# Taking full tiles and end tiles of the expert stage in turns from place 36 on

## The chip, the cores and the metric

The kernel runs on one core of one Trainium2 chip. The metric is the device time of one execution in microseconds; a smaller number is better. The engines are TensorE (PE, with its weight loads shown as PEld), VectorE (DVE), ScalarE (ACT), GpSimd (POOL) and SyncE (SP), which only issues transfers.

## What is computed

A graph network layer on 32 graphs of 256 nodes (8192 tokens, 128 features) is followed by a feed-forward layer with 8 experts, of which each token uses two. The second half is what the change touches:

```python
logits = jnp.einsum('bsd,de->bse', xn, Wr) + br
top_vals, top_idx = jax.lax.top_k(logits, K)            # K = 2
w = jax.nn.softmax(top_vals, axis=-1)
w_full = jnp.einsum('bsk,bske->bse', w, jax.nn.one_hot(top_idx, E, dtype=w.dtype))
for e in range(E):                                       # E = 8, H = 256, D = DOUT = 128
    h = jax.nn.gelu(jnp.einsum('bsd,dh->bsh', xn, W1[e]) + b1[e], approximate=False)
    y_e = jnp.einsum('bsh,hd->bsd', h, W2[e]) + b2[e]
    y = y + y_e * w_full[..., e, None]
```

## The kernel before

**Routing.** A token's two experts make a class; there are 28 classes. In the first stage (16 groups of 512 tokens) the graph layer and the router run, and every token's row (normalised features, residual, shares, its own number) is scattered to `rows_dram`, sorted by class. Each class then consists of full tiles of 128 rows and one end tile, which is filled up with idle rows.

**Places.** The expert stage goes through 92 places, one tile each: places 0 to 63 are slots for full tiles (`NT`), places 64 to 91 the end tiles of the 28 classes (`NC`). The first 20 (`EARLY`) start while the last two groups are still being routed; from place 20 on the tables are complete. The class of an end tile is known when the program is built. The class of a full tile is data: four of them are packed in one 24-bit word, which PE, ACT and DVE load into a register at every fourth full tile (`value_load`), and from which `expert` computes the addresses of weights, biases and shares with register instructions.

**One step.** All engines run a loop over steps, each written out in the program's order:

- SP loads the rows of place i into one of 26 buffers (line 428), once the result of place i - 26 has been sent. Behind every second load from place 21 to 47 it also writes the idle rows of one class's end tile (`fill_end`, line 432); those of the first 14 classes are written before place 20. Before place 64 it waits for all 28 (`fill_sent`).
- PE transposes the tile of place i (line 785), does the wide product of place i - 2 (four matmuls, line 805) and the narrow one of place i - 4 (four matmuls, line 822). There are three banks for narrow products, so the narrow product of place m waits for the result of place m - 3.
- ACT copies the weights of a full tile to fixed buffers (lines 946 and 950), moves the transposed tile (line 955) and applies gelu (line 962). An end tile needs no copy, since PE reads its weights in place.
- DVE, in this order: first bias of place i (line 1545), first product of place i - 4 (line 1559), second bias of place i (line 1566), second product of place i - 4 (line 1573, the result). The word for place i is loaded at line 1540, that for place i - 4 at line 1551; as 4 is also the number of tiles in a word, both loads fall in the same step.
- POOL scatters the result to `out` (line 572) and, up to place 85, clears a scratch tile behind it (line 528).

Of the kernel before, what the change touches and what calls it, by code (L numbers as in the profile page):

```python
# [8 lines left out]
P = 128  # L9
# [5 lines left out]
NT = NTOK // P  # L15
# [7 lines left out]
NC = len(PAIRS)  # L23
# [29 lines left out]

BACK = D + E

XR, XD, AR, RO, HR = 6, 3, 3, 8, 8
STEPS = NG + 3
RING, SENDS = 26, 18
# [40 lines left out]
    return rows  # L99


def expert(words, i, width, low):

    if i >= NT:
        return PAIRS[i - NT][0 if low else 1] * width
    word = words[i // PER_WORD % 2]
    at = 6 * (i % PER_WORD) + (0 if low else 3)
    shift = width.bit_length() - 1 - at
    if shift > 0:
        taken = (word & (E - 1) << at) << shift  # L110
    else:
        taken = (word >> -shift) & (E - 1) * width
    return taken.with_bounds(min_val=0, max_val=(E - 1) * width)


def build(nc, x, x_t, adj_t, eps, gw1, gb1, rms_w, gw2, gb2, gamma, beta, wr, br, w1, b1, w2, b2,
          fixed_in, idle_in, out):
    fixed_at = constants()[1]
    with ExitStack() as ctx:
# [3 lines left out]
        def sem(name):  # L123
            return ctx.enter_context(nc.semaphore(name))
# [211 lines left out]
        columns_turned = sem("columns_turned")  # L336
        table_ready = sem("table_ready")
        ends_ready = sem("ends_ready")
        fill_sent = sem("fill_sent")
        idle_sent = sem("idle_sent")  # L340

        rows_here = [sem(f"rows_here{k}") for k in range(RING)]
# [45 lines left out]

        def highs_placed(i):

            return sum(high_by_gpsimd(m) == high_by_gpsimd(i) for m in range(i + 1))

        block = ctx.enter_context(nc.Block())

        @block.sync
        def _(sp):
            def load_features(g):
                if g >= XD:
                    sp.wait_ge(x2_ready, g - XD + 1)
                sp.dma_start(x_d[:, g % XD], x_t[:, g * GT:(g + 1) * GT]).then_inc(x_d_in[g % XD], 16)  # L400

            for g in range(NG):
                if g == XR:
                    for dst, src in expert_loads:
                        sp.dma_start(dst, src).then_inc(weights_in, 16)
                if g >= XR:
                    sp.wait_ge(xn1_ready, g - XR + 1)
                if g == 2:
                    sp.wait_ge(adj_in[1], 16)
                sp.dma_start(x_tok[:, g % XR], x_view[g]).then_inc(x_in[g % XR], 16)  # L410
                if g >= AR:
                    sp.wait_ge(agg_done, g - AR + 1)
                if g == 1:
                    sp.wait_ge(adj_in[0], 16)
                sp.dma_start(adj[:, g % AR], adj_view[g]).then_inc(adj_in[g % AR], 16)
                if g >= 4:
                    load_features(g - 4)
            for g in range(NG - 4, NG):
                load_features(g)

            def load_rows(i):
                if i < NT:
                    start = sp.value_load(first_row[0:1, i:i + 1], min_val=0, max_val=IDLE + (NC - 1) * P)
                else:
                    start = sp.value_load(left_row[0:1, i - NT:i - NT + 1], min_val=0, max_val=IDLE + (NC - 1) * P)
                if i >= RING:
                    sp.wait_ge(result_sent[(i - RING) % SENDS], 16 * ((i - RING) // SENDS + 1))
                sp.dma_start(rows_in[:, i % RING], rows_dram[bass.ds(start, P), :]).then_inc(rows_here[i % RING], 16)

            def fill_end(c):  # L430
                end = sp.value_load(end_row[0:1, c:c + 1], min_val=0, max_val=IDLE + (NC - 1) * P)
                sp.dma_start(rows_dram[bass.ds(end, P), :], idle_in[c * P:(c + 1) * P]).then_inc(fill_sent, 16)

            sp.wait_ge(table_ready, 1)
            for k, n in enumerate(sent_before(KNOWN)):
                sp.wait_ge(rows_sent[k], 16 * TPG * n)
            for i in range(EARLY):
                load_rows(i)

            sp.wait_ge(ends_ready, 1)
            for c in range(NC // 2):
                fill_end(c)
            sp.wait_ge(table_ready, 3)
            sp.wait_ge(idle_sent, 16)
            for k, n in enumerate(sent_before(NG - 1)):
                sp.wait_ge(rows_sent[k], 16 * TPG * n)
            for i in range(EARLY, NT):
                load_rows(i)  # L450
                if i % 2 and i - EARLY < NC:
                    fill_end(NC // 2 + (i - EARLY) // 2)
            sp.wait_ge(fill_sent, 16 * NC)
            for i in range(NT, TILES):
                load_rows(i)

        @block.gpsimd
        def _(pool):
# [163 lines left out]
        def _(pe):  # L622
# [157 lines left out]
            def tile_step(step):  # L780
# [7 lines left out]
                if (i := tile_at(step, WIDE_LAG)) is not None:  # L788
                    pe.wait_ge(xg_t_ready, i + 1)
                    if (m := before_in_bank(H_BANKS, i)) is not None:  # L790
                        pe.wait_ge(gelu_done, m + 1)
                    for w, now in enumerate((w1_low, w1_high)):
                        if i >= NT:
                            now_at = expert({}, i, HE, w == 0)
                            w1_now = w1_sb[:, now_at:now_at + HE]
                        else:
                            w1_now = now[:, i % 4]
                            if w == 0:
                                pe.wait_ge(low_placed, i + 1)
                            elif high_by_gpsimd(i):  # L800
                                pe.wait_ge(high_placed2, highs_placed(i))
                            else:
                                pe.wait_ge(high_placed, highs_placed(i))
                        for c in range(HCE):
                            last = pe.matmul(h_ps(i)[:, w * HCE + c], w1_now[:, c * P:(c + 1) * P], xg_t[:, i % 4],  # L805
                                             start=True, stop=True)
                    last.then_inc(h_done, 1)
                    tail(step, 1)
                if (i := tile_at(step, NARROW_LAG)) is not None:
                    if i < NT and i % PER_WORD == 0:  # L810
                        words[i // PER_WORD % 2] = pe.value_load(word[0:1, i // PER_WORD:i // PER_WORD + 1], min_val=0,
                                                                 max_val=2 ** 24 - 1)
                    pe.wait_ge(gelu_done, i + 1)
                    if (m := before_in_bank(Y_BANKS, i)) is not None:
                        pe.wait_ge(result_ready, m + 1)
                    for w in range(2):
                        if i < EARLY:
                            bias_at = expert(words, i, D, w == 0)
                            pe.matmul(y_ps(i)[:, w], bias_sel[:], b2_parts[:, bass.ds(bias_at, D)], start=True, stop=False)
                        at = expert(words, i, HE, w == 0)  # L820
                        for c in range(HCE):
                            last = pe.matmul(y_ps(i)[:, w], hidden_e[:, i % 4, w * HCE + c],  # L822
                                             w2_sb[:, bass.ds(at + c * D, D)], start=(c == 0 and i >= EARLY),
                                             stop=(c == HCE - 1))
                    last.then_inc(y_done, 1)
                    tail(step, 2)
# [13 lines left out]
        def _(act):  # L840
# [97 lines left out]
            def place_weights(i):  # L938
                if i >= 4:
                    act.wait_ge(h_done, i - 3)  # L940
                if i < NT:
                    if i % PER_WORD == 0:
                        words[i // PER_WORD % 2] = act.value_load(word[0:1, i // PER_WORD:i // PER_WORD + 1],
                                                                  min_val=0, max_val=2 ** 24 - 1)
                    at = expert(words, i, HE, True)
                    nc.scalar.activation(w1_low[:, i % 4], w1_sb[:, bass.ds(at, HE)], ACT.Copy
                                         ).then_inc(low_placed, 1)
# [40 lines left out]
        def _(dve):  # L988
# [544 lines left out]
            def tile_step(step):  # L1533
# [2 lines left out]
                    i = None  # L1536
                if i is not None:
                    rows = rows_in[:, i % RING]
                    if i < NT and i % PER_WORD == 0:
                        words[i // PER_WORD % 2] = dve.value_load(word[0:1, i // PER_WORD:i // PER_WORD + 1],  # L1540
                                                                  min_val=0, max_val=2 ** 24 - 1)
                    dve.wait_ge(rows_here[i % RING], 16 * (i // RING + 1))
                    if i >= AHEAD:
                        dve.wait_ge(result_ready, i - AHEAD + 1)
# [2 lines left out]
                                                   rows[:, X2_AT:X2_AT + D], ALU.mult, ALU.add).then_inc(based, 1)  # L1547
                tail(step, 0)
                if j is not None:
                    if j < NT and j % PER_WORD == 0:  # L1550
                        done_words[j // PER_WORD % 2] = dve.value_load(word[0:1, j // PER_WORD:j // PER_WORD + 1],
                                                                       min_val=0, max_val=2 ** 24 - 1)
                    done = rows_in[:, j % RING]
                    if j >= EARLY:
                        dve.wait_ge(base_done, j - EARLY + 1)
# [65 lines left out]
```

## Time and profile before

| | |
|---|---|
| median of 3 runs | 411.95 us (411.73 to 412.13) |
| time of the profiled execution | 411.64 us |
| its span, first to last instruction | 409.9 us |
| mean granted TensorE clock | 0.995 |
| TensorE busy (weight loads) | 382.9 us (326.3 us) |
| VectorE busy | 301.2 us |
| ScalarE busy | 277.7 us |
| GpSimd busy | 314.2 us |

The profiled execution is 0.31 us below the median, and 1.7 us of it lie outside the span. A busy TensorE says only that some matmul is in flight; whether it runs at its pace is read from the starts of equal instructions one tile apart.

### The profile page before, as it was taken

Reading aid. Unit: us, or ns where it says so; the run is one execution under the profiler, and the core shown is the slowest. Engines: PE = TensorE matmul, PEld = TensorE weight load, DVE = VectorE, ACT = ScalarE, POOL = GpSimd, SP = SyncE. Lnnn points to the kernel's source line nnn. Section 1 sums busy time; section 2 is a strip of 40 time slices with the busy share of each in tenths; the row PEclk is TensorE's granted clock in tenths of the full one; section 3 lists DMA queues with packets and bytes.
Section 4 is the critical chain, followed back from the end, with each engine's and each line's share of the span. In section 5 each row is a group of like instructions: output and inputs, shape, how many; then the busy total and the mean of one; then the engine's idle time right before and its main releaser. Section 6 shows DMA issues by size and latency. Waiting matters only on the chain. (4 is left out here: it accounts for less than half of the span.)

```text
span 409.9 us, 11327 instructions
## 1 busy us (share of the span) xinstructions
PE 382.9 (93%) x2598; PEld 326.3 (80%) x2598; DVE 301.2 (73%) x1290; ACT 277.7 (68%) x653; POOL 314.2 (77%) x440
## 2 busy tenths in 40 slices
PE   1899999999999999999789996999999999999994
PEld 1467777767777777777569996999999899999993
DVE  5687789999999999998865752566666666765562
ACT  1377777787778898779878554677777776555540
POOL 1223378877787899888888879997787677999984
PEclk9999999999999999999999999899999999999999
DMA  7879974444423442221266355555555544331111
GB/s 227 259 242 337 338 232 137 141 144 142 139 88 115 156 144 79 76 69 55 68 157 180 111 156 140 158 150 153 145 153 156 156 124 110 108 87 40 38 38 38
DMA packets 43472, 57.25 MB, mean 140 GB/s; under 512 B 6224, under 2 KB 36176, under 8 KB 42768
## 3 DMA queue, kind: packets, MB, share of 16 engines
q1 hardware_dynamic: 35200, 36.74, 32.4%
q0 software_dynamic: 6096, 18.52, 12.9%
q10 hardware_dynamic: 2112, 1.27, 1.1%
q8 instruction: 24, 0.39, 0.4%
q14 instruction: 40, 0.33, 0.3%
HBM read 41.80 MB, written 22.31 MB: 156 GB/s over the span
## 5 line engine op out<-in xcount | busy, mean ns | idle before, releaser
L572 POOL DMA_INDIRECT out<-result,rows_in x92 | 90.3, 981 | 27.8 <-DVE result L1573 15.8
L822 PE MATMUL banks<-w_sb,hidden_e 128*128 (+1 forms) x736 | 102.7, 281 | 2.8 <-DVE result L1573 2.4
L822 PEld LDWEIGHTS banks<-w_sb,hidden_e 128*128 128x128 f32 x736 | 92.2, 193 | 4.7 <-issue 4.2
L962 ACT ACTIVATE hidden_e<-banks 128x512 f32<-128x512 f32 x92 | 54.9, 597 | 45.4 <-PE banks L805 43.6
L515 POOL DMA_INDIRECT rows_dram<-rows_out,row_of x64 | 65.3, 1021 | 13.4 <-issue 10.6
L649 PE MATMUL banks<-gw_sb,agg 128*128 128x512 f32 x128 | 65.2, 595 | 0.9 <-DVE gw_sb L1013 0.9
L673 PE MATMUL banks<-hidden_t,gw_sb 128*128 128x256 f32 x256 | 62.3, 386 | 1.7 <-ACT hidden_t L885 1.7
L528 POOL MEMSET space<- 128x620 f32 x100 | 63.0, 630 | 0.1
L673 PEld LDWEIGHTS banks<-hidden_t,gw_sb 128*128 128x128 f32 x256 | 46.4, 190 | 16.1 <-ACT hidden_t L885 7.3
L1108 DVE TENSOR_TENSOR hidden<-banks,rms_bc 128x512 f32<-128x512 f32 x64 | 43.8, 685 | 15.3 <-ACT hidden L870 15.1
L955 ACT ACTIVATE xg_t<-banks,ones 128x128 f32<-128x128 f32 x92 | 33.3, 362 | 22.0 <-PE banks L785 21.9
L878 ACT ACTIVATE hidden<-hidden,rrms 128x512 f32<-128x512 f32 x64 | 45.8, 717 | 0.1
L1559 DVE SCALAR_TENSOR_TENSOR acc<-banks,rows_in,acc 128x128 f32<-128x128 f32 x72 | 25.2, 351 | 26.9 <-PE banks L822 19.5
L870 ACT ACTIVATE hidden<-banks 128x512 f32<-128x512 f32 x64 | 38.2, 596 | 9.6 <-PE banks L649 7.8
L637 PE MATMUL banks<-adj,xn 128*128 128x256 f32 x128 | 32.3, 398 | 9.2 <-DVE xn L1089 9.2
L885 ACT ACTIVATE hidden_t<-banks 128x512 f32<-128x512 f32 x64 | 38.0, 594 | 3.1 <-PE banks L660 2.9
L805 PE MATMUL banks<-xg_t,w_low 128*128 128x128 f32 x256 | 39.7, 278 | 0.0
L660 PEld LDWEIGHTS banks<-fixed,hidden 128*128 128x128 f32 x256 | 30.4, 141 | 11.5 <-issue 6.6
L805 PE MATMUL banks<-xg_t,w_high 128*128 128x128 f32 x256 | 39.1, 275 | 0.0
L660 PE MATMUL banks<-fixed,hidden 128*128 128x128 f32 x256 | 38.9, 275 | 0.1
L1545 DVE SCALAR_TENSOR_TENSOR acc<-b_bc,rows_in 128x128 f32<-128x128 f32 x72 | 25.1, 349 | 15.9 <-DVE result L1573 13.4
L469 POOL TENSOR_TENSOR rstd<-var,minus_half 128x4 f32<-128x4 f32 x16 | 16.9, 1056 | 26.0 <-DVE var L1081 25.7
(148 smaller groups left out, 741.2 us busy)
## 6 DMA issues: line engine op xcount, KB each, us to landing
rows_in<-rows_dram SPq DMA_DIRECT2D x92, 132.5 KB, 2.3
adj<-adj_t SPq DMA_DIRECT2D x16, 512.0 KB, 5.0
x_tok<-x SPq DMA_DIRECT2D x16, 256.0 KB, 6.1
x_d<-x_t SPq DMA_DIRECT2D x16, 256.0 KB, 4.8
rows_dram<-idle_in POOLq DMA_DIRECT2D x1, 3710.0 KB, 13.9
rows_dram<-idle_in SPq DMA_DIRECT2D x28, 132.5 KB
out<-result,rows_in POOLq DMA_INDIRECT x92
w_sb<-w SPq DMA_DIRECT2D x1, 1024.0 KB, 8.3
```

The source lines that it names most:

```text
L515: nc.gpsimd.indirect_dma_start(out=rows_dram, out_offset=bass.IndirectOffsetOnAxis(ap=row_of[:, g * TPG + t:g * TPG + t + 1], axis=0), in_ ...
L528: nc.gpsimd.memset(space[:], 0.0).then_inc(spaced, 1)
L572: nc.gpsimd.indirect_dma_start(out=out, out_offset=bass.IndirectOffsetOnAxis(ap=rows_in[:, i % RING][:, IDX_AT:IDX_AT + 1].bitcast(U32), a ...
L649: pe.matmul(hid_ps[:, n % 3], agg[:, g % 2, t * P:(t + 1) * P], gw1_sb[:], start=True, stop=True).then_inc(hid_done, 1)
L660: last = pe.transpose(hidt_ps[t % 2][:, c * P:(c + 1) * P], hidden[:, n % HR, c * P:(c + 1) * P], ident)
L673: last = pe.matmul(z_ps[:, cols], gw2_sb[:, c], hidden_t[:, g % 2, c, cols], start=(c == 0), stop=(c == HC1 - 1))
L805: last = pe.matmul(h_ps(i)[:, w * HCE + c], w1_now[:, c * P:(c + 1) * P], xg_t[:, i % 4], start=True, stop=True)
L822: last = pe.matmul(y_ps(i)[:, w], hidden_e[:, i % 4, w * HCE + c], w2_sb[:, bass.ds(at + c * D, D)], start=(c == 0 and i >= EARLY), stop=( ...
L870: nc.scalar.activation(hidden[:, n % HR], hid_ps[:, n % 3], ACT.Square, scale=H1 ** -0.5, accum_out=sumsq[:, g % 2, t:t + 1]).then_inc(sum ...
L878: nc.scalar.activation(hidden[:, n % HR], hidden[:, n % HR], ACT.Silu, scale=rrms[:, g % 2, t:t + 1]).then_inc(silu_done, 1)
L962: nc.scalar.activation(hidden_e[:, i % 4], h_ps(i), ACT.Gelu).then_inc(gelu_done, 1)
L1108: nc.vector.tensor_tensor(hidden[:, n % HR], hid_ps[:, n % 3], rms_bc[:], ALU.mult).then_inc(weighted, 1)
```

## The change

The order of the tiles is mapped: places 0 to 35 are full tiles as before; from place 36 (`TURNS`) on, even places take the full tiles 36 to 63 and odd places the end tiles 0 to 27. A word is loaded when a full tile with a number divisible by four comes up, which is at every eighth place from 36 on. The waits for placed weights count full tiles only. The wait for the idle rows is split in halves: the first 14 classes' before the load of place 37, the others' before that of place 65.

```diff
+TURNS = TILES - 2 * NC
+def tile_of(i):
+    if i < TURNS:
+        return i
+    k = (i - TURNS) // 2
+    return NT + k if (i - TURNS) % 2 else TURNS + k
 def expert(words, i, width, low):
+    i = tile_of(i)
     if i >= NT:
...
-        fill_sent = sem("fill_sent")
+        fill_sent = [sem(f"fill_sent{k}") for k in range(2)]
...
-            return sum(high_by_gpsimd(m) == high_by_gpsimd(i) for m in range(i + 1))
+            return sum(high_by_gpsimd(m) == high_by_gpsimd(i) for m in range(i + 1) if tile_of(m) < NT)
+        def lows_placed(i):
+            return sum(tile_of(m) < NT for m in range(i + 1))
+        def new_word(i):
+            t = tile_of(i)
+            return t // PER_WORD if t < NT and t % PER_WORD == 0 else None
...
             def load_rows(i):
-                if i < NT:
-                    start = sp.value_load(first_row[0:1, i:i + 1], min_val=0, max_val=IDLE + (NC - 1) * P)
+                t = tile_of(i)
+                if t < NT:
+                    start = sp.value_load(first_row[0:1, t:t + 1], min_val=0, max_val=IDLE + (NC - 1) * P)
...
-            for i in range(EARLY, NT):
+            for i in range(EARLY, TILES):
+                for k in range(2):
+                    if tile_of(i) == NT + k * NC // 2:
+                        sp.wait_ge(fill_sent[k], 16 * (NC // 2))
                 load_rows(i)
                 if i % 2 and i - EARLY < NC:
                     fill_end(NC // 2 + (i - EARLY) // 2)
-            sp.wait_ge(fill_sent, 16 * NC)
-            for i in range(NT, TILES):
-                load_rows(i)
...
-                        if i >= NT:
+                        if tile_of(i) >= NT:
...
-                                pe.wait_ge(low_placed, i + 1)
+                                pe.wait_ge(low_placed, lows_placed(i))
...
-                    if i < NT and i % PER_WORD == 0:
-                        words[i // PER_WORD % 2] = dve.value_load(word[0:1, i // PER_WORD:i // PER_WORD + 1],
-                                                                  min_val=0, max_val=2 ** 24 - 1)
+                    if (k := new_word(i)) is not None:
+                        words[k % 2] = dve.value_load(word[0:1, k:k + 1], min_val=0, max_val=2 ** 24 - 1)
```

The last replacement is made in the same way for PE, for ACT and for the second load on DVE.

## Rows read from the trace of the kernel before

**Rows 1.** Busy us (x instructions) of PE, PEld, DVE, ACT, POOL; then clock, DMA share, GB/s.

```profile
268.19:287.15 18.96, 18.96 (x173) 18.96 (x171) 13.05 (x38) 14.82 (x40) 15.73 (x21) 1.00 0.54 151
...
287.15:345.19 58.04, 55.37 (x479) 53.98 (x477) 39.24 (x113) 42.17 (x112) 44.55 (x56) 1.00 0.53 143
...
345.19:396.38 51.19, 51.19 (x462) 51.19 (x461) 33.02 (x114) 26.04 (x54) 46.53 (x58) 1.00 0.23 67
```

**Rows 2.** Timeline of TensorE: starts of single transposes, one at each place.

```profile
287.15 0.27 PE L785 MATMUL banks<-fixed,rows_in 128*128 128x128 f32 x1
...
292.84 0.27 PE L785 MATMUL banks<-fixed,rows_in 128*128 128x128 f32 x1
...
295.11 0.27 PE L785 MATMUL banks<-fixed,rows_in 128*128 128x128 f32 x1
...
297.16 0.27 PE L785 MATMUL banks<-fixed,rows_in 128*128 128x128 f32 x1
...
300.96 0.27 PE L785 MATMUL banks<-fixed,rows_in 128*128 128x128 f32 x1
...
303.58 0.27 PE L785 MATMUL banks<-fixed,rows_in 128*128 128x128 f32 x1
...
305.48 0.27 PE L785 MATMUL banks<-fixed,rows_in 128*128 128x128 f32 x1
...
345.19 0.27 PE L785 MATMUL banks<-fixed,rows_in 128*128 128x128 f32 x1
...
396.38 0.27 PE L785 MATMUL banks<-fixed,rows_in 128*128 128x128 f32 x1
```

**Rows 3.** Waits between 285 and 345 us: in total, times, longest.

```profile
PE banks L822 <- DVE result L1573: 2.4, 5, 0.5
```

**Rows 4.** Timeline of VectorE, steps in which both tiles are full.

```profile
293.33 0.35 DVE L1573 SCALAR_TENSOR_TENSOR result<-banks,rows_in,acc 128x128 f32<-128x128 f32 x1
...
333.28 0.35 DVE L1545 SCALAR_TENSOR_TENSOR acc<-b_bc,rows_in 128x128 f32<-128x128 f32 x1 [0.62 <-DVE result L1573]
...
334.19 0.35 DVE L1559 SCALAR_TENSOR_TENSOR acc<-banks,rows_in,acc 128x128 f32<-128x128 f32 x1 [0.56 <-issue]
...
335.54 0.35 DVE L1545 SCALAR_TENSOR_TENSOR acc<-b_bc,rows_in 128x128 f32<-128x128 f32 x1 [0.17 <-DVE result L1573]
...
337.32 0.35 DVE L1545 SCALAR_TENSOR_TENSOR acc<-b_bc,rows_in 128x128 f32<-128x128 f32 x1 [0.21 <-DVE result L1573]
...
339.10 0.35 DVE L1545 SCALAR_TENSOR_TENSOR acc<-b_bc,rows_in 128x128 f32<-128x128 f32 x1 [0.21 <-DVE result L1573]
...
341.67 0.35 DVE L1545 SCALAR_TENSOR_TENSOR acc<-b_bc,rows_in 128x128 f32<-128x128 f32 x1 [1.00 <-DVE result L1573]
```

**Rows 5.** Timeline of VectorE, one step in which both are end tiles.

```profile
353.36 0.34 DVE L1545 SCALAR_TENSOR_TENSOR acc<-b_bc,rows_in 128x128 f32<-128x128 f32 x1
...
354.54 0.34 DVE L1545 SCALAR_TENSOR_TENSOR acc<-b_bc,rows_in 128x128 f32<-128x128 f32 x1
```

**Rows 6.** VectorE's register load of line 1551: ns min/median/max, first and last start.

```profile
L1551 DVEq TENSOR_LOAD <-word x16: 298/304/661, 213.5 to 348.8; - x16
```

**Rows 7.** Timeline of SyncE: start, length of the run of issues, their count.

```profile
232.33 18.29 SPq L432 DMA_DIRECT2D rows_dram<-idle_in  x14
...
280.24 1.45 SPq L428 DMA_DIRECT2D rows_in<-rows_dram  x2
...
300.38 0.59 SPq L432 DMA_DIRECT2D rows_dram<-idle_in  x1
```

**Rows 8.** Timeline of GpSimd: two sends of results.

```profile
380.46 1.10 POOL L572 DMA_INDIRECT out<-result,rows_in  x1 [0.17 <-DVE result L1573]
...
394.83 0.97 POOL L572 DMA_INDIRECT out<-result,rows_in  x1 [0.17 <-issue]
```

**Rows 9.** Timeline of the end: last result and last send.

```profile
404.29 0.35 DVE L1573 SCALAR_TENSOR_TENSOR result<-banks,rows_in,acc 128x128 f32<-128x128 f32 x1
...
405.89 0.97 POOL L572 DMA_INDIRECT out<-result,rows_in  x1 [0.30 <-DMA out<-result,rows_in]
```

More of the change, by code:

```diff
@@ L421, in load_rows @@
             def load_rows(i):
-                if i < NT:
-                    start = sp.value_load(first_row[0:1, i:i + 1], min_val=0, max_val=IDLE + (NC - 1) * P)
+                t = tile_of(i)
+                if t < NT:
+                    start = sp.value_load(first_row[0:1, t:t + 1], min_val=0, max_val=IDLE + (NC - 1) * P)
                 else:
-                    start = sp.value_load(left_row[0:1, i - NT:i - NT + 1], min_val=0, max_val=IDLE + (NC - 1) * P)
+                    start = sp.value_load(left_row[0:1, t - NT:t - NT + 1], min_val=0, max_val=IDLE + (NC - 1) * P)
                 if i >= RING:
@@ L431, in fill_end @@
                 end = sp.value_load(end_row[0:1, c:c + 1], min_val=0, max_val=IDLE + (NC - 1) * P)
-                sp.dma_start(rows_dram[bass.ds(end, P), :], idle_in[c * P:(c + 1) * P]).then_inc(fill_sent, 16)
+                sp.dma_start(rows_dram[bass.ds(end, P), :], idle_in[c * P:(c + 1) * P]).then_inc(fill_sent[c // (NC // 2)], 16)
             sp.wait_ge(table_ready, 1)
@@ L809, in tile_step @@
                 if (i := tile_at(step, NARROW_LAG)) is not None:
-                    if i < NT and i % PER_WORD == 0:
-                        words[i // PER_WORD % 2] = pe.value_load(word[0:1, i // PER_WORD:i // PER_WORD + 1], min_val=0,
-                                                                 max_val=2 ** 24 - 1)
+                    if (k := new_word(i)) is not None:
+                        words[k % 2] = pe.value_load(word[0:1, k:k + 1], min_val=0, max_val=2 ** 24 - 1)
                     pe.wait_ge(gelu_done, i + 1)
@@ L940, in place_weights @@
                     act.wait_ge(h_done, i - 3)
-                if i < NT:
-                    if i % PER_WORD == 0:
-                        words[i // PER_WORD % 2] = act.value_load(word[0:1, i // PER_WORD:i // PER_WORD + 1],
-                                                                  min_val=0, max_val=2 ** 24 - 1)
+                if tile_of(i) < NT:
+                    if (k := new_word(i)) is not None:
+                        words[k % 2] = act.value_load(word[0:1, k:k + 1], min_val=0, max_val=2 ** 24 - 1)
                     at = expert(words, i, HE, True)
@@ L1538, in tile_step @@
                     rows = rows_in[:, i % RING]
-                    if i < NT and i % PER_WORD == 0:
-                        words[i // PER_WORD % 2] = dve.value_load(word[0:1, i // PER_WORD:i // PER_WORD + 1],
-                                                                  min_val=0, max_val=2 ** 24 - 1)
+                    if (k := new_word(i)) is not None:
+                        words[k % 2] = dve.value_load(word[0:1, k:k + 1], min_val=0, max_val=2 ** 24 - 1)
                     dve.wait_ge(rows_here[i % RING], 16 * (i // RING + 1))
@@ L1549, in tile_step @@
                 if j is not None:
-                    if j < NT and j % PER_WORD == 0:
-                        done_words[j // PER_WORD % 2] = dve.value_load(word[0:1, j // PER_WORD:j // PER_WORD + 1],
-                                                                       min_val=0, max_val=2 ** 24 - 1)
+                    if (k := new_word(j)) is not None:
+                        done_words[k % 2] = dve.value_load(word[0:1, k:k + 1], min_val=0, max_val=2 ** 24 - 1)
                     done = rows_in[:, j % RING]
```

## The prediction

> **What bounds the kernel now.** I read the page first: TensorE is busy 93% of the span, which hides whether it runs at its pace. So the next view is the timeline of TensorE, of the transposes alone, since there is one for each place. The last one, at 396.38 us, is place 91, and 27 before it, at 345.19, is place 64, the first end tile [rows 2]. That is 51.19 us for 27 places, 1.896 us each. Another 28 back stands place 36, at 287.15: 58.04 us for 28 full tiles, 2.073 each. The reader is to see two regimes on one engine. In the second, weight loads fill the whole stretch (51.19 of 51.19 us) at granted clock 1.00 [rows 1]: TensorE's own pace. Full tiles alone can reach it too: the stretch before place 36 (268.19 to 287.15) holds ten places in 18.96 us, at the same clock [rows 1]. So a full tile isn't dearer for TensorE, and after place 36 something holds it up: 58.04 - 28 x 1.896 = 4.95 us.
>
> The view of the waits names DVE's result as what TensorE's narrow products waited for, five times, 2.4 us [rows 3]; the weight loads behind such a wait are late as well, which that line doesn't count. The starts show where: place 39 to 40 takes 2.27 us instead of 1.896, 40 to 41 takes 2.05, 43 to 44 takes 2.62, and then 44 to 45 is 1.90 again [rows 2]. In step 39 the narrow product of place 35 is due, which needs the result of place 32; in step 43 that of place 39, which needs result 36. Both results come from steps in which DVE loads its two words.
>
> DVE's timeline gives the price. A step with two full tiles and no word takes 1.78 us (337.32 to 339.10). The one with the words has 0.62 us of idle time before line 1545 and 0.56 before line 1559, where the others have 0.21 and next to nothing. Four steps with one word step take 341.67 - 333.28 = 8.39 us [rows 4], that is 2.10 a tile, against TensorE's 4 x 1.896 = 7.58. DVE is the bound among full tiles, by its register work, although it counts as busy for only 39.24 of 58.04 us. It starts with some places in hand (three banks), so TensorE feels it only from step 39 on. Among end tiles a step of DVE takes 354.54 - 353.36 = 1.18 us [rows 5], and it waits for TensorE in every one. So DVE binds for 28 places and idles for the next 28.
>
> **The change, part by part.** *DVE.* No instruction on data is added or removed; the register work of 28 full tiles is spread over 56 places. The lag of four places between the two halves of a step is even, so from place 40 on both halves are full or both are end tiles. Eight steps are then four full ones, with two word loads as now, and four end ones: 8.39 + 4 x 1.18 = 13.11 us. TensorE needs 8 x 1.896 = 15.17. DVE gains 2.06 us in eight steps, 0.26 a step, where it now loses 0.20 among full tiles. The two loads no longer meet: place 36, 44, 52 and 60 bring line 1540's, and steps 40, 48, 56 line 1551's, so each word step has one of about half the extra time; only in step 36 do both fall together (tile 36 and tile 32). One load takes 304 ns on DVE [rows 6].
>
> *Where the gain begins.* Steps up to 36 are the same instructions. Step 36 has both loads, and result 32 is ready as late as before (started 293.33 [rows 4]), so the 2.27 us before place 40 stays: place 40 starts at 295.11 again. From there the next word step must not stall. DVE's steps 37 and 39 have one full half and one end half (between 1.18 and 1.78, middle 1.48), 38 is full, 40 is full with one word (1.78 and half of the two loads' 1.0, so 2.3): 7.04 us from result 32 to result 36. TensorE takes 7.58 over four places, so result 36 is 0.5 us earlier against its need than result 32, which was late by 2.27 - 1.90 = 0.37. It now takes DVE 8.39. No stall is left after 40; the little one to place 41 (2.05 - 1.90 = 0.15) stays or goes.
>
> *TensorE.* From place 40 to 91 there are 51 intervals. At 1.896: 295.11 + 96.7 = 391.81 us for the last transpose instead of 396.38, 4.57 earlier. If the small stall stays, 4.42; if the first goes as well, 4.95.
>
> *ACT.* It copies weights for every second place only. Ten full tiles in a row at TensorE's pace cost it 14.82 us busy in 18.96 [rows 1], so it isn't the bound even at twice that density.
>
> *SP.* Its queue keeps the order of loads and fills; only the row addresses differ, and the waits for the idle rows move. The wait before place 37 is for the 14 fills issued from 232.33 to 250.62, thirty microseconds earlier. The other 14 end with the one at 300.38 [rows 7], behind the load of place 47, and are asked for before that of place 65, which can't be issued before result 39 is out anyway. Cost nothing; what hides it: the pair of loads 36 and 37 is issued at 280.24, so place 37's at about 281.0, lands 2.3 us later by the page, and is used at 287.15 + 1.90 = 289.05. 5.7 us of cover.
>
> *POOL.* It sends one result a place. 0.17 idle, 0.97 send and 0.63 clearing (the page's mean for line 528) make 1.77 us [rows 8], below 1.896. It keeps up. In one stretch, though, the send takes 1.10 us, and then 1.90 is just TensorE's pace.
>
> The Trainium skill, "SBUF — State Buffer", section "Who interferes with whom", says that a DVE instruction with two inputs in SBUF contends with a GpSimd instruction that reads SBUF, and not with one that only writes. DVE's bias steps are of that kind, and they will come more evenly than now. By the row of 0.97 the sum has no term for POOL; by the rule POOL would be as in the stretch of 1.10, which the rival below prices. This trace bears the rule out no further than 1.10 beside 0.97.
>
> *The end.* Now 13.5 us lie between the last transpose and the end of the span; the last result starts at 404.29 and its send at 405.89 [rows 9]. After the change places 88 and 90 are full, so DVE does register work for two of its four instructions there: between nothing (it waits for TensorE before them) and half of 1.78 - 1.18 = 0.3 each. I take 0.1 in all.
>
> Sum: 411.64 - 4.57 + 0.1 = 407.17 us for a profiled execution, and 0.31 more to the median of the runs: 407.5 us.
>
> **The rivals.**
>
> *The lag stays for some rounds.* If mixed steps cost DVE as much as full ones (1.78), result 36 comes 7.64 us after result 32 and the late place isn't made good; one or two of the stalls of 2.62 - 1.90 = 0.72 are left, at 43 to 44 and at 51 to 52. For it: the pieces of idle time that the profile puts down to nothing. Against it: 0.26 gained a step. Time 408.9 with two left.
>
> *It is TensorE's own word load.* TensorE loads every word too, and this count stays. Then seven stalls of 0.72 stay, and nothing is gained: 412. Against it: its load for tile 40 is in step 44, and place 44 to 45 takes 1.90 us; the stall stands one step earlier. Also its loads for tiles 24 and 28, in steps 28 and 32, fell in the stretch at full pace [rows 1].
>
> *POOL has no slack.* If its sends take 1.10 us from place 40 on, its period is 1.90, it never works off a lag, and up to one period stands before the last sends: between 407.5 and 409.3, some 408.5. Against it: it went back to 0.97 by itself [rows 8], and the last six sends have no clearing behind them. The skill's rule named under POOL speaks for it.
>
> *Slower: an end tile's load blocks SP.* All loads from 37 on and the second 14 fills stand behind the wait before place 37. It decides only if the first fills land after 281.0 + 5.7 = 286.7, and makes the kernel slower if after 286.7 + 4.5 + 0.8 = 292.0: 41 us after the last was issued. The page's slowest transfer of idle rows, 3710 KB, takes 13.9. If it happened, at 44 us say, 415.
>
> **How the numbers follow.** My forecast, own range 406.6 to 408.3 (bounds: both stalls gone, 407.1, less some noise; small stall left and 0.6 at the end, 408.2): 0.75. Lag for some rounds 0.11, POOL 0.08, TensorE's own load 0.03, blocked SP 0.03. The range takes in the first three as far as 409.2: 406.4 to 409.2. Within 0.2% of 411.95 is 411.1 to 412.8, about what a measurement can tell from no change. Faster 0.94, same 0.03, slower 0.03.
>
> **What would show it.** Right: transposes 1.90 us apart from place 40 to 91, the last at about 391.8; no wait of line 822 for line 1573 after about 296 us; DVE waiting for line 822 from some place after 44 on; word steps with one long idle piece instead of two. Wrong: intervals of 2.6 every eight places (TensorE's own load, or ACT late with its copies), POOL never waiting for a result in the last 30 us, or a hole at place 37 with "rows_in" as its releaser. What would make it wrong most easily: a cost of changing between kinds of tiles that no row here shows, as none here has both kinds in turn; DVE's mean step of 1.64 would pass 1.896 only if each change cost over 0.26 us.

## The result, and the profile after

The changed kernel took 408.07 us (median of 6 runs, 407.16 to 409.66) against 412.21 for the kernel before (6 runs, 411.73 to 412.53): ratio 0.991, 95% interval 0.9891 to 0.9928. Forecast were 407.5 us in a range of 406.4 to 409.2. It is faster. These six runs scatter more than those of before; in a later round (the last table of the experiments) the two kernels scatter alike, over 3.0 and 2.8 us.

The profiled execution took 408.06 us, with a span of 406.2. The windows of the changed kernel (columns as in [rows 1]) show the same three kinds of stretch; line 806 is now the transpose, 842 the narrow product, 1563, 1576, 1583 and 1590 DVE's four instructions in their order, 593 the send.

```profile
264.55:287.83 23.28, 23.00 (x206) 22.82 (x205) 14.97 (x44) 18.19 (x49) 21.12 (x28) 1.00 0.54 150
287.83:341.36 53.53, 53.41 (x478) 53.22 (x477) 37.31 (x118) 34.61 (x85) 48.56 (x61) 1.00 0.55 154
295.86:392.55 96.69, 96.69 (x870) 96.69 (x868) 65.70 (x209) 62.73 (x153) 84.73 (x106) 1.00 0.39 111
```

The last one is places 40 to 91: weight loads fill all of its 96.69 us. The timeline of TensorE, transposes alone (places 35, 36, 39, 40, 91):

```profile
285.40 0.27 PE L806 MATMUL banks<-fixed,rows_in 128*128 128x128 f32 x1
...
287.83 0.27 PE L806 MATMUL banks<-fixed,rows_in 128*128 128x128 f32 x1
...
293.58 0.27 PE L806 MATMUL banks<-fixed,rows_in 128*128 128x128 f32 x1
...
295.86 0.27 PE L806 MATMUL banks<-fixed,rows_in 128*128 128x128 f32 x1
...
392.55 0.27 PE L806 MATMUL banks<-fixed,rows_in 128*128 128x128 f32 x1
```

392.55 - 295.86 = 96.69 us for 51 places, 1.896 each: none of the stalls of [rows 2] is left behind place 40. The 28 places from 36 to 64 take 341.36 - 287.83 = 53.53 us instead of 58.04. Place 39 to 40 takes 2.28, as before. New is place 35 to 36: 2.43 us instead of 1.90.

The waits of the changed kernel between 285 and 345 us have no row any more in which line 842 waits for DVE's result [rows 3]. That alone proves little, since the two stalls before places 36 and 40 lie in this window and the view puts them down to nothing ("issue", the second line below); the starts above are what shows them, and that none follows. The order of waiting has turned round, DVE waits for TensorE:

```profile
DVE acc L1576 <- PE banks L842: 4.8, 10, 0.9
...
PEld banks L842 <- issue: 0.8, 2, 0.5
```

DVE's own steps while it catches up (timeline of VectorE; steps 41 to 44 begin with these rows, 41 and 43 are end steps, 42 a full one):

```profile
301.13 0.34 DVE L1563 SCALAR_TENSOR_TENSOR acc<-b_bc,rows_in 128x128 f32<-128x128 f32 x1
...
302.31 0.35 DVE L1563 SCALAR_TENSOR_TENSOR acc<-b_bc,rows_in 128x128 f32<-128x128 f32 x1
...
303.81 0.34 DVE L1563 SCALAR_TENSOR_TENSOR acc<-b_bc,rows_in 128x128 f32<-128x128 f32 x1
...
305.41 0.35 DVE L1563 SCALAR_TENSOR_TENSOR acc<-b_bc,rows_in 128x128 f32<-128x128 f32 x1 [0.48 <-issue]
```

1.18 us for an end step, as in [rows 5]; 303.81 - 302.31 = 1.50 us for a full one, less than the 1.78 of [rows 4]. The word for step 44 is loaded in the 0.48 us before its first instruction, alone: the other load is gone from that step.

One send that took longer, and the end (the last result and its send; before: [rows 9]):

```profile
391.32 1.11 POOL L593 DMA_INDIRECT out<-result,rows_in  x1 [0.72 <-DVE result L1590]
...
400.75 0.35 DVE L1590 SCALAR_TENSOR_TENSOR result<-banks,rows_in,acc 128x128 f32<-128x128 f32 x1
...
402.23 0.98 POOL L593 DMA_INDIRECT out<-result,rows_in  x1 [0.30 <-issue]
```

From the last transpose to the end of the span pass 406.2 - 392.55 = 13.65 us, before 13.5.

### The profile page after: what moved, and what is told of

Its sections match the earlier page's. It is cut to its first block and busy times, and to the rows that moved or that the text cites. A ratio compares the mean times of both kernels' runs of the same rounds, so it can differ in the third digit from the quotient of the medians.

```text
span 406.2 us, 11327 instructions
## 1 busy us (share of the span) xinstructions
PE 381.3 (94%) x2598; PEld 325.6 (80%) x2598; DVE 300.4 (74%) x1290; ACT 277.6 (68%) x653; POOL 314.4 (77%) x440
## 5 line engine op out<-in xcount | busy, mean ns | idle before, releaser
L536 POOL DMA_INDIRECT rows_dram<-rows_out,row_of x64 | 65.5, 1023 | 13.5 <-issue 10.7
L658 PEld LDWEIGHTS banks<-adj,xn 128*128 128x128 f32 x128 | 25.2, 199 | 14.3 <-issue 8.1
```

Of the source, the lines that this page charges most:

```text
L536: nc.gpsimd.indirect_dma_start(out=rows_dram, out_offset=bass.IndirectOffsetOnAxis(ap=row_of[:, g * TPG + t:g * TPG + t + 1], axis=0), in_ ...
L658: last = pe.matmul(agg_ps[:, b * NODES:(b + 1) * NODES], xn1[:, g % 2, 2 * b + c], adj[:, g % AR, 2 * b + c], start=(c == 0), stop=(c == 1))
```

## The experiments

Most runs are compared by TensorE's transposes rather than by their times. The times carry a scatter that arises ahead of the places concerned: from place 8 to place 24, where the last groups are routed and the tables built, the profiles below take between 41.3 and 45.5 us, whatever the kernel. The kernel before itself took 412.21, 414.26, 408.99 and 412.46 us in the four rounds of runs (6, 7, one and 11 executions), so a time is compared only with that of the kernel before in the same round. b_peload (round of 414.26) and a_pad1, a_pad3, a_endsfirst and a_blocks14 (round of 408.99) ran once each. All sums in this table are differences of starts of transposes in the profiled execution; the last column is from the last transpose to the end of the span. At TensorE's pace places 24 to 91 would take 67 x 1.896 = 127.0 us.

| kernel | time of this execution | places 8 to 24 | 24 to 36 | 36 to 64 | 64 to 91 | 24 to 91 | behind |
|---|---|---|---|---|---|---|---|
| before | 411.64 | 41.88 | 22.75 | 58.04 | 51.19 | 131.98 | 13.5 |
| changed | 408.06 | 41.76 | 23.28 | 53.53 | 51.19 | 128.00 | 13.65 |
| changed, again (a_again) | 409.06 | 41.74 | 24.32 | 53.61 | 51.18 | 129.11 | 13.7 |
| before, words loaded once (b_reuse) | 406.94 | 42.83 | 22.96 | 53.09 | 51.18 | 127.23 | 13.5 |
| the same again (b_reuse_again) | 406.33 | 41.58 | 22.75 | 53.15 | 51.19 | 127.09 | 13.4 |
| before, more loads on TensorE (b_peload) | 415.96 | 45.53 | 23.23 | 57.87 | 51.23 | 132.33 | 13.7 |
| changed, words loaded once (a_reuse) | 409.85 | 44.72 | 23.24 | 53.08 | 51.19 | 127.51 | 13.5 |
| turns from place 20 (a_turns20) | 408.71 | 43.03 | 22.75 | 53.08 | 51.19 | 127.02 | 14.0 |
| 1 more in each end step (a_pad1) | 406.58 | 41.54 | 22.75 | 53.46 | 51.19 | 127.40 | 13.6 |
| 3 more in each end step (a_pad3) | 408.28 | 42.33 | 22.75 | 53.45 | 51.19 | 127.39 | 13.9 |
| 28 end tiles, then 28 full (a_endsfirst) | 411.43 | 42.36 | 22.75 | 53.08 | 52.11 | 127.94 | 16.6 |
| blocks of 14 (a_blocks14) | 408.59 | 41.66 | 22.75 | 56.07 | 51.18 | 130.00 | 13.5 |
| all together (a_best) | 406.12 | 41.26 | 23.34 | 53.09 | 51.18 | 127.61 | 13.4 |

**Is it DVE's register work? (b_reuse)** The order stays as before; only the word of a full tile is kept from the step in which DVE first needs it.

```diff
                         words[i // PER_WORD % 2] = dve.value_load(...)
+                        kept[i // PER_WORD] = words[i // PER_WORD % 2]
...
                     if j < NT and j % PER_WORD == 0:
-                        done_words[j // PER_WORD % 2] = dve.value_load(...)
+                        if j < EARLY:
+                            done_words[j // PER_WORD % 2] = dve.value_load(...)
+                        else:
+                            done_words[j // PER_WORD % 2] = kept[j // PER_WORD]
```

> The kernel before, but from place 20 on VectorE loads each word once: the word that line 1540 loads for place i is kept for the same tile four steps later, so line 1551's load goes. Theory (VectorE's register work bounds the full tiles): a group of four full steps falls from 8.39 us by about 0.5 to 7.9, still above TensorE's 7.58; the stalls of 2.6 us at every fourth place fall to 1.9 to 2.3, places 36 to 64 take about 54.5 instead of 58.0 us, and the time is 2.5 to 3.5 us below the kernel before. Rival (TensorE's own word load, or anything outside VectorE, makes the stalls): no change within 0.3 us.

Measured: places 36 to 64 in 53.09 us, all intervals from place 34 to 91 at 1.90; 408.09 us (median of 4) against 414.26 of the kernel before on that chip, ratio 0.9872 (0.9825 to 0.9918). The rival is out: nothing but DVE's register work was touched, and every stall behind place 34 went (one of 0.2 us is left ahead of it, before place 32). I had the size wrong, since I took one load off and nothing more. The sequencer's records of line 1559 before and of its successor, line 1563, in the second run of this kernel:

```profile
L1559 DVEq ALU_OP  x112: 40/45/57, 216.4 to 353.4; - x112
```

```profile
L1563 DVEq ALU_OP  x35: 40/45/57, 216.2 to 264.3; - x35
```

112 register instructions became 35, and the last of these is at 264.3 us, before any of the full tiles concerned; line 1577 (the result) went from 128 to 40. With one register for both halves, the addresses computed for a tile in its first half serve again in its second. Four results in a row (timeline of VectorE, the second run):

```profile
292.36 0.35 DVE L1577 SCALAR_TENSOR_TENSOR result<-banks,rows_in,acc 128x128 f32<-128x128 f32 x1
...
293.87 0.34 DVE L1577 SCALAR_TENSOR_TENSOR result<-banks,rows_in,acc 128x128 f32<-128x128 f32 x1
...
295.90 0.34 DVE L1577 SCALAR_TENSOR_TENSOR result<-banks,rows_in,acc 128x128 f32<-128x128 f32 x1
...
297.82 0.35 DVE L1577 SCALAR_TENSOR_TENSOR result<-banks,rows_in,acc 128x128 f32<-128x128 f32 x1
```

The first pair lies in steps without a word and without a wait: 1.51 us for a full step instead of 1.78. The last pair spans a step with its word, 1.92 us; between them DVE waits for TensorE. That makes 3 x 1.51 + 1.92 = 6.45 us for four, below TensorE's 7.58 by far, where I had expected 7.9, and the time fell by 6 us on that chip instead of 2.5 to 3.5. The profiles show 4.75 us of it (places 24 to 91, 131.98 to 127.23); they don't show where the rest lies.

**Is it TensorE's own load of the word? (b_peload)**

```diff
                         words[i // PER_WORD % 2] = pe.value_load(word[0:1, i // PER_WORD:i // PER_WORD + 1], ...)
+                    if EARLY <= i < NT and i % PER_WORD == 2:
+                        words[i // PER_WORD % 2] = pe.value_load(word[0:1, i // PER_WORD:i // PER_WORD + 1], ...)
```

> The kernel before with one more load of the same word into a register on TensorE for every four full tiles from place 20 on (11 more loads). Theory: TensorE's own load is hidden, the intervals stay at 2.6 us once in four places and the time stays within 0.5 us of the kernel before. Rival (TensorE's own word load makes the stall): a second stall of about 0.7 us in each group, 4 to 7 us slower.

The eleven loads were made, 303 ns each:

```profile
L814 PEldq TENSOR_LOAD <-word x11: 297/303/308, 271.0 to 352.6; - x11
```

Places 24 to 91 took 132.33 us against 131.98 before, and 36 to 64 even 57.87 against 58.04. Seven stalls more would have been 5 us. TensorE's load is hidden. (Its time of 415.96 is high because places 8 to 24 took 3.7 us longer; that part is the same code.) This kernel, in the order of before, also shows a stall, 2.38 us from place 35 to 36, so such a stall doesn't need the turns. It has added loads ahead of that place, though, so it is not quite the kernel before.

**What is left for DVE in the changed kernel? (a_reuse, a_turns20)** The first keeps the words as above in the changed kernel. The second begins the mixing at place 20 (`tile_of(i)` then returns `ORDER[i]`, here and in the orders further down):

```diff
-TURNS = TILES - 2 * NC
+FULLS, ENDS = list(range(EARLY, NT)), list(range(NT, TILES))
+ORDER = list(range(EARLY))
+while FULLS or ENDS:
+    late = len(ENDS) * (NT - EARLY) > len(FULLS) * NC
+    ORDER.append((ENDS if late or not FULLS else FULLS).pop(0))
```

> The changed kernel with the same saving on VectorE. Theory: VectorE is no bound from place 40 on, so nothing is gained there; only the stalls before place 36 and 40 (2.43 and 2.28 instead of 1.90 us) go, since VectorE goes through places 20 to 36 with less register work: 0.5 to 1.0 us below the changed kernel. Rival (VectorE still bounds the stage in turns): 2 us or more below.

> The changed kernel with the mixing begun at place 20 instead of 36: 44 full and 28 end tiles spread evenly over places 20 to 91. Theory: VectorE never falls behind, the stalls at places 36 and 40 go, every interval from about place 25 on is 1.90 us: 0.8 to 1.1 us below the changed kernel. Rival (those two intervals have another cause, such as instruction fetch): no change. Rival (irregular order costs something): slower than the changed kernel.

Measured: 408.0 us (ratio 0.9849, 0.9801 to 0.9896) and 407.3 us (0.9836, 0.9792 to 0.9881), both against 414.26. In both profiles places 36 to 64 take 53.08 us, which is 28 x 1.896, so the stall before place 40 is gone as expected, and so is that before place 36. But a_reuse has two others further ahead, 2.06 us before place 29 and 2.22 before place 31, which make its 23.24 us for places 24 to 36. By places 24 to 91 a_reuse is 0.5 us below the changed kernel and a_turns20 1.0. With turns from place 20 places 24 to 91 take 127.02 us, TensorE's pace throughout. Behind the last transpose a_turns20 takes 14.0 us, 0.4 more than the changed kernel: its place 91 is a full tile.

**How much slack has DVE in turns? (a_pad1, a_pad3)** In every end step behind place 40 (26 of them, one more than the expectation counts) DVE gets 1 or 3 instructions more:

```diff
+                if i is not None and i > 40 and tile_of(i) >= NT:
+                    ...
+                    for n in range(3):
+                        last = nc.vector.scalar_tensor_tensor(pad[:, n], b2_bc[:, 0:D], rows[:, W_AT:W_AT + 1],
+                                                              rows[:, X2_AT:X2_AT + D], ALU.mult, ALU.add)
```

> The changed kernel with one more VectorE instruction (the form of line 1545, static addresses, result never used) in each of the 25 steps from 43 on whose tile is an end tile. Theory: VectorE needs 13.11 us for eight steps where TensorE needs 15.17; one more instruction an end step adds 4 x 0.26 = 1.04, 14.15 in all, still below. Places 24 to 91 take 128.0 us as in the changed kernel, within 0.3. Rival (VectorE sets the pace in the stage in turns): 25 x 0.26 = 6.5 us longer.

> The same with three such instructions in each end step. Theory: 13.11 + 12 x 0.26 = 16.23 us for eight steps, 1.06 more than TensorE's 15.17; over the 49 places from 43 on 6.5 us, less the places that VectorE may lag behind (three banks, 2 to 4 us): places 24 to 91 take 2.5 to 5 us longer than in the changed kernel, and TensorE's intervals are uneven (1.90 and over 2.1) again in the last third. If VectorE has more slack than I reckon, no change.

One more costs nothing, as expected (127.40). Three more cost nothing either (127.39), where I had expected 2.5 to 5 us. The timeline of VectorE in that run, the starts of steps 46 and 54 and between them the three instructions of step 47 in one row:

```profile
310.43 0.35 DVE L1565 SCALAR_TENSOR_TENSOR acc<-b_bc,rows_in 128x128 f32<-128x128 f32 x1
...
312.19 0.89 DVE L1573 SCALAR_TENSOR_TENSOR pad<-b_bc,rows_in 128x128 f32<-128x128 f32 x3
...
325.25 0.35 DVE L1565 SCALAR_TENSOR_TENSOR acc<-b_bc,rows_in 128x128 f32<-128x128 f32 x1
```

Eight steps take 325.25 - 310.43 = 14.82 us, with twelve instructions more at 0.26, and fit below TensorE's 15.17. Without them it is 11.7 us, not my 13.11. The surplus is in the full steps: 1.50 us in turns, 1.78 among themselves. Probably the register instructions of a full step run while the four instructions of the end step before it, which need none, are still being worked off; that reading no run tests.

**Is it turns that matter, or DVE's lag? (a_blocks14, a_endsfirst)** The two orders, with the numbers written out:

```diff
-TURNS = TILES - 2 * NC
+ORDER = list(range(36)) + list(range(64, 92)) + list(range(36, 64))      # a_endsfirst
+ORDER = [*range(50), *range(64, 78), *range(50, 64), *range(78, 92)]     # a_blocks14
```

> The changed kernel with another order from place 36 on: all 28 end tiles, then full tiles 36 to 63. Theory: the 28 end tiles run at 1.90 and let VectorE catch up; the full tiles then start without a lag, VectorE loses 0.2 us a tile, and TensorE feels it only after its slack of some 3 to 4 us is used, after 15 to 20 tiles: 1.5 to 3 us of stalls at the end, 1.5 to 3 us slower than the changed kernel in places 24 to 91, and 2 to 3.5 faster than before. Rival (a stretch of full tiles costs the same wherever it stands): as slow as before, 4 us slower than the changed kernel.

> From place 36 on 14 full, 14 end, 14 full, 14 end tiles. Theory: the first 14 full tiles follow 16 others, so the lag is there already, and their stalls stay (about 0.75 at every fourth place, 2.5 us in all); in the second block VectorE starts without a lag and 14 x 0.2 = 2.8 us stays within the slack, no stall. Places 24 to 91 take 1.5 to 2.5 us longer than in the changed kernel. Rival (what matters is only that the kinds take turns one by one): 4 us longer.

In blocks of 14 the first block of full tiles (places 36 to 49) has the stalls of before: 2.27, 2.05, 2.63, 2.79 and 2.69 us at places 40, 41, 44, 48 and 52, 3.0 us in all over the pace. The second block of 14 full tiles has none. Places 24 to 91 take 2.0 us longer than in the changed kernel, as expected. With the end tiles first, full tiles run at 1.90 for 20 places and stall at 84, 88 and 89, for 0.9 us together; 1.5 to 3 was too much. But 3 us came where I had not looked. The end of that run:

```profile
394.59 1.28 PE L839 MATMUL banks<-w_sb,hidden_e 128*128 x8 [0.39 <-DVE result L1587]
...
400.26 1.15 PE L839 MATMUL banks<-w_sb,hidden_e 128*128 x8 [0.71 <-DVE result L1587]
...
401.86 1.15 PE L839 MATMUL banks<-w_sb,hidden_e 128*128 x8 [0.45 <-DVE result L1587]
...
404.07 0.35 DVE L1587 SCALAR_TENSOR_TENSOR result<-banks,rows_in,acc 128x128 f32<-128x128 f32 x1 [0.29 <-DVE acc L1573]
...
405.69 0.98 POOL L590 DMA_INDIRECT out<-result,rows_in  x1 [0.31 <-DMA out<-result,rows_in]
```

The last narrow products wait for DVE's results (0.39, 0.71, 0.45), and 16.6 us pass behind the last transpose instead of 13.5. A lag that is within the slack of three banks costs nothing in mid-stage and is paid nearly in full at the end: result 87 starts 6.45 us after the transpose of place 91, in the kernel before 2.69, and the last result comes 3.1 us later behind that transpose than there. So the rival (a stretch of full tiles costs the same wherever it stands) falls for the places. With the end counted, places 24 to 91 and what is behind them take 144.5 us, 2.9 more than in the changed kernel, as expected, but only 1.0 less than in the kernel before, where 2 to 3.5 were expected. The time itself shows no gain at all: 411.43 us, against 408.99 for the kernel before in the same round, one execution each, which the scatter of places 8 to 24 can cover.

**Side by side on one chip (a_again, b_reuse_again, a_best).** a_best has turns from place 20, words loaded once, and end tiles in the last four places.

```diff
+ORDER, LAST = list(range(EARLY)), 4
+while FULLS:
+    late = (len(ENDS) - LAST) * (NT - EARLY) > len(FULLS) * (NC - LAST)
+    ORDER.append((ENDS if late else FULLS).pop(0))
+ORDER += ENDS
```

> The changed kernel once more, unaltered, on one chip with the next two. Expected: about 1% below the kernel before, as in its first runs; in its profile places 40 to 91 at 1.90 us each, places 24 to 91 in 127.4 to 128.1 us.

> The order before with every word loaded once on VectorE, unaltered from its first run. If the whole gain is VectorE's register work, this kernel and the changed one come out the same within 0.5 us, without any new order; if the new order does something of its own, the changed kernel is faster.

> All together: the mixing from place 20 on, every word loaded once on VectorE, and the last four places end tiles. Places 24 to 91 at TensorE's pace, 127.0 us, and 13.5 us behind them: 0.6 to 1.0 us below the changed kernel; more can't come from VectorE, since TensorE is the bound from place 24 on.

| kernel | median | runs | ratio to before (412.46) |
|---|---|---|---|
| changed, again | 408.68 | 407.38 to 410.39 | 0.9909 (0.9883 to 0.9935) |
| before, words loaded once | 406.62 | 406.27 to 406.71 | 0.9858 (0.9837 to 0.9880) |
| all together | 406.33 | 406.03 to 407.76 | 0.9861 (0.9839 to 0.9883) |

The order before, with the words loaded once, is 2 us faster than the changed kernel, not within 0.5 us of it as expected. a_best is 2.3 us below it, not 0.6 to 1.0. The changed kernel's profile says where it loses them in that execution. TensorE's transposes of places 35 and 36 in that run:

```profile
286.03 0.27 PE L806 MATMUL banks<-fixed,rows_in 128*128 128x128 f32 x1
...
288.75 0.27 PE L806 MATMUL banks<-fixed,rows_in 128*128 128x128 f32 x1
```

2.72 us for one place; 25 to 26 takes 2.16, 31 to 32 takes 2.31, 39 to 40 takes 2.36. These are stalls of full tiles in places 20 to 39, ahead of the turns: 24 to 36 takes 24.32 us instead of 22.75, and 24 to 91 takes 129.11 where at most 128.1 was expected. Loading the words once takes most of them away there too (24 to 36 takes 22.96, 22.75 and, in a_reuse, 23.24 us). Against it the new order on top gives nothing that can be measured (0.9858 and 0.9861), since both run at TensorE's pace from place 24 on but for 0.1 and 0.6 us. Both are faster than the two kernels of this study.

## Why the prediction was right, and where it was off

**The bound and the gain.** DVE's register work held TensorE up among full tiles, and 28 places in turns took 53.53 us instead of 58.04. b_reuse shows the cause, since it changes that work alone; b_peload excludes TensorE's own load; a_pad1 and a_pad3 show that DVE isn't the bound in turns. Places 40 to 91 took 96.69 us, forecast were 96.7.

**The step that was off: "place 40 starts at 295.11 again".** It started at 295.86. Of the 0.75 us, 0.15 were there at place 24 already (264.55 instead of 264.40). The other 0.60 lie between 24 and 40: the stall of 0.53 before place 36, and 0.07 behind it. The reasoning was that the instructions up to step 36 are the same, so the times are. But DVE is behind by another amount in each execution, and the first stall falls on place 36 or 40 accordingly. Up to result 18 the two profiles agree: it starts 2.63 us ahead of the transpose of place 25 in both. The difference is one piece of idle time in step 23, before DVE's first product of place 19 (timelines of VectorE, before and after):

```profile
264.93 0.35 DVE L1559 SCALAR_TENSOR_TENSOR acc<-banks,rows_in 128x128 f32<-128x128 f32 x1 [0.35 <-PE banks L822]
```

```profile
265.67 0.35 DVE L1576 SCALAR_TENSOR_TENSOR acc<-banks,rows_in 128x128 f32<-128x128 f32 x1 [0.94 <-PE banks L842]
```

TensorE isn't what it waited for: the last matmuls of that narrow product started at 263.90 and 264.05 and took 0.66 us, so DVE's product started 0.37 us behind them before and 0.96 after. In a_again the same piece is 1.84 us long, in a_pad1 and a_pad3 it is as short as before. What holds DVE there stays open. TensorE doesn't make it good, since DVE has no slack among full tiles, so the 0.6 us are still there at result 28:

```profile
285.31 0.35 DVE L1573 SCALAR_TENSOR_TENSOR result<-banks,rows_in,acc 128x128 f32<-128x128 f32 x1
```

```profile
286.05 0.35 DVE L1590 SCALAR_TENSOR_TENSOR result<-banks,rows_in,acc 128x128 f32<-128x128 f32 x1
```

It started 0.06 us after the transpose of place 35 (285.25) before the change, and 0.65 after it (285.40) behind the change. TensorE's narrow product, due at that step, then came 0.53 late. The stall before place 40 itself came out as forecast (2.28 us; result 32 was as late against its need as before). In a_pad1 and a_pad3, which are the changed kernel up to place 40, no stall fell on 36 and places 24 to 91 took 127.4 us: the forecast's own figure, 30.71 + 96.7. In a_again it was 129.1. So the term should have been a range: 0.4 us of stalls before place 40 in the best profile, 2.1 in the worst. How much of the scatter of the runs comes from there and how much from places 8 to 24 can't be told, as only two executions of the changed kernel were profiled.

**The end.** I took 0.1 us for full tiles in places 88 and 90; it was 0.15 (13.65 against 13.5). a_turns20 with a full tile in the last place pays more.

**DVE's budget in turns.** 13.11 us for eight steps was mis-sized: 14.82 - 3.12 = 11.7 by a_pad3. It didn't change the forecast, as both are below 15.17.

**The sum.** 407.17 forecast for a profiled execution, 408.06 measured: 0.75 at place 40, 0.05 at the end, and 0.1 outside the span (1.86 us instead of 1.74). That the time itself lies in the range is in part luck: it counts from 411.95 us, and the kernel before took 412.21 beside the changed one, but 414.26 and 408.99 in other rounds. The difference doesn't hang on that: 4.1 us in this round and 3.8 in the round of a_again, forecast were 4.45.

**A row misread.** The prediction says that among end tiles DVE waits for TensorE in every step. The step it shows, from 353.36 to 354.54, has no such wait; the first is at 356.83, 11.6 us behind the transpose of place 64, and until then DVE works off its lag. The 1.18 us are its own pace for that reason, so the sum isn't hurt.

**The rivals.** *The lag stays for some rounds:* not behind place 40; DVE made step 37 to 40's results in 300.86 - 294.08 = 6.78 us where 7.04 were reckoned. Its like, stalls ahead of the turns, is what a_again shows. *TensorE's own load:* out by b_peload. *POOL has no slack:* out; in the changed kernel its sends took 0.97 us but for a few at 1.06 to 1.11, so that the contention which the Trainium skill ("SBUF — State Buffer", "Who interferes with whom") allows for shows itself, if it is the cause, in single instructions only. Among end tiles alone whole stretches are at 1.10 (all sends from 311.7 to 340.2 us in a_endsfirst), and the places kept TensorE's pace there too. DVE with 78 instructions more (a_pad3) left the places at TensorE's pace, with 13.9 us at the end instead of 13.65. *A blocked SP queue:* no hole at place 37; the interval was 1.96 us.

## What to carry to other kernels

Where two kinds of work have different bounds, taking them in turns hides the cost of the dearer one; look first whether it can be taken away, as here a word loaded and decoded twice on the engine that sets the pace. A busy share of 68% doesn't say that an engine has time left: count its period from start to start, register instructions included. A lag within the buffers is free in mid-stage and is mostly paid at the end, so dear work should not stand last.

## What the runs showed of the hardware that was not expected

- A full step of DVE costs 1.78 us among full steps, 1.50 in turns with steps that have no register work, and 1.51 with half of its address computations gone. Twelve more instructions in eight steps fit in.
- The compiled program shares address computations between two uses of one loaded register: 112 and 128 register instructions fell to 35 and 40 by loading the word once.
- The passage from routing to the expert stage (places 8 to 24) takes from 41.3 to 45.5 us in thirteen profiles, on code that is the same up to place 20: 14 to 15 took 3.6 us in the profile of before, 5.7 after the change, and 3.1 to 6.1 in others. This is as large as the whole effect of the change. Its cause stays open; no run here was made for it.
- DVE can stand idle for 0.6 to 1.5 us more in a single step and not in the same step of another execution, with TensorE's product long there (0.94 and 1.84 us in step 23 of two profiles of the changed kernel, 0.35 in that of before). Where DVE is the bound, such a piece stays as a lag. Its cause stays open.
